# Attention over a graph batch: row factors split in fp16, turned by DMA and spread by TensorE with a constant; k's sums by VectorE

## The reference

```python
h = maximum(layernorm(x), 0)
q, k, v = heads(h @ Wq.T), heads(h @ Wk.T), heads(h @ Wv.T)
a = einsum('bhnd,bhmd->bhnm', q, k) * D ** -0.5 + 2 * adj      # adj is passed twice as bias
row_nonzero = any(a != 0, axis=-1)
p = softmax(where(row_nonzero, a, -inf));  p = where(isnan(p), 0, p)
o = einsum('bhnm,bhmd->bhnd', p, v)
out = x + o.reshape(B, N, D) @ Wo.T
```

## Time and profile before

| | |
|---|---|
| median of 3 runs | 1008.4 us (1008.09 to 1008.94) |
| the profiled execution | 1011.04 us, of which its span (first to last instruction) is 1009.2 us |
| PE busy | 967.0 us, 96% |
| ACT busy | 926.8 us, 92% |
| POOL busy | 861.7 us, 85% |
| DVE busy | 853.0 us, 85% |
| DMA, share of 16 engines | 98.1% |
| mean granted clock of TensorE | 0.988 of 2.4 GHz |

### The profile page before, as it was taken

How to read it: one execution, slowest core, us unless ns; L and a number is a source line. 1 busy time by engine, 2 the same in 40 slices (tenths; PEclk the granted TensorE clock), 3 DMA queues, 4 the chain that set the end, 5 groups by cost and what they waited for, 6 DMA issues and landing times.

```text
span 1009.2 us, 33752 instructions
## 1 busy us (share of the span) xinstructions
PE 967.0 (96%) x11596; PEld 666.3 (66%) x11596; DVE 853.0 (85%) x3090; ACT 926.8 (92%) x3025; POOL 861.7 (85%) x936
## 2 busy tenths in 40 slices
PE   6788999999999999999999999999999999999965
PEld 5566766676776667677666777666677766667632
DVE  6778988889898888989888898988889898888863
ACT  3399999999999999999999999999999999999992
POOL 1178989899988989998898999989899988989894
PEclk9899999999999999999999999999999999999988
DMA  6088999999999999999999999999999999999995
GB/s 250 11 145 144 190 188 188 183 193 200 179 190 189 189 188 192 187 199 184 185 182 194 188 201 187 185 194 175 193 192 195 177 196 183 190 188 176 172 178 117
DMA packets 569579, 182.59 MB, mean 181 GB/s; under 512 B 542784, under 2 KB 550976, under 8 KB 569408
## 3 DMA queue, kind: packets, MB, share of 16 engines
q1 hardware_dynamic: 569408, 180.43, 98.1%
HBM read 29.36 MB, written 16.78 MB: 46 GB/s over the span
## 4 chain that ended last, share of the span: by engine, by line
PE 58%; DVE 27%; issue 8%; ACT 5%; POOL 2%; DMA 1%; DVEq 0%; POOLq 0%; ACTq 0%; SPq 0%
PE ps L978 36%; DVE logits L690 14%; PE ps L1046 8%; PE ps L996 7%; DVE stats L595 4%; PE ps L861 3%; ACT probs L509 3%; DVE q_lo L753 2%; DVE o_norm L720 2%; PE ps L1022 1%; DVE some L708 1%; DVE w_max L610 1%; ACT p L522 1%; PE ps L950 1%; POOL p L411 1%
## 5 line engine op out<-in xcount | busy, mean ns | idle before, releaser
L411 POOL TENSOR_TENSOR p<-probs,p 128x512 f16<-128x512 f32 x512 | 586.5, 1162 | 95.8 <-ACT p L522 95.6
L509 ACT ACTIVATE probs<-logits,row_min 128x256 f32<-128x256 f32 x1024 | 514.3, 513 | 1.3 <-DVE row_min L690 1.3
L690 DVE CUSTOM_DVE_ANT_0 logits<-ps,adj_s,sigma 128x256 f32<-128x256 f32 x1024 | 438.0, 475 | 9.8 <-PE ps L996 9.7
L522 ACT ACTIVATE p<-probs 128x512 f16<-128x512 f32 x512 | 324.2, 633 | 0.0
L978 PE MATMUL ps<-ht_hi,w_hi 128*128 128x256 f16 x1024 | 280.9, 274 | 6.4 <-DVE w_lo L650 1.9
L978 PE MATMUL ps<-ht_lo,w_hi 128*128 128x256 f16 x1024 | 280.2, 274 | 0.0
L978 PE MATMUL ps<-ht_hi,w_lo 128*128 128x256 f16 x1024 | 280.1, 274 | 0.0
L509 ACT ACTIVATION_READ_ACCUMULATOR probs<-logits,row_min 128x1 f32 x1024 | 211.4, 206 | 0.0
L978 PEld LDWEIGHTS ps<-ht_hi,w_hi 128*128 128x128 f16 x1024 | 100.4, 98 | 34.3 <-DVE q_lo L753 11.4
L978 PEld LDWEIGHTS ps<-ht_lo,w_hi 128*128 128x128 f16 x1024 | 100.6, 98 | 14.5
L978 PEld LDWEIGHTS ps<-ht_hi,w_lo 128*128 128x128 f16 x1024 | 100.6, 98 | 12.0
(11 more groups left out here) (88 smaller groups left out, 1654.9 us busy)
## 6 DMA issues: line engine op xcount, KB each, us to landing
xs<-in_x SPq DMA_DIRECT2D x32, 512.0 KB, 4.5
out<-xs SPq DMA_DIRECT2D x64, 256.0 KB, 2.9
adj_raw<-in_adj SPq DMA_DIRECT2D x32, 256.0 KB, 3.6
pt<-p SPq DMA_TRANSPOSE x256, 4.1
w_nat<-p SPq DMA_TRANSPOSE x256, 3.3
w_nat<-in_L_gnn_Wq SPq DMA_DIRECT2D x1, 1024.0 KB, 6.3
w_nat<-in_L_gnn_Wk SPq DMA_DIRECT2D x1, 1024.0 KB, 9.1
w_nat<-in_L_gnn_Wv SPq DMA_DIRECT2D x1, 1024.0 KB, 11.2
```

Source lines behind the costliest of these rows:

```text
L411: g.tensor_tensor(p16[:, c % 2, k, 1], probs[:, h % 4].rearrange("p u n -> p (u n)"), p16[:, c % 2, k, 0], ALU.subtract).then_inc(p_split, 1)
L509: e = a.activation(probs[:, h % 4, u, :], logits[:, h % 4, u, :], ACT.Exp, bias=row_min[:, t.par(d), u, h:h + 1], scale=-1.0, accum_out=ro ...
L522: a.activation(p16[:, c % 2, k, 0], probs[:, h % 4].rearrange("p u n -> p (u n)"), ACT.Copy)\
L690: v.tensor_tensor_reduce(out=logits[:, h % 4, u, :], in0=ps[:, S_BANK + h % HC, N * u:N * u + N], in1=adj_s[:, t.par(d), u, :], scale=sigm ...
```

## The change

The row factors are finished by VectorE. `invert` runs twice for each batch, not four times (steps 7 and 15), over eight heads: `recip`, `some`, their product times 2^14 (`factor`), its fp16 part, and the fp16 rest, each waiting for the one before. Both parts lie side by side in `factor16[:, p, :]` (128 columns of fp16, of which 64 stay zero). A DMA transpose turns this into `factor16_t`, and TensorE multiplies it with a constant `spread` matrix (2^-14 where feature row and factor belong together), which adds the two parts and spreads them in the same matmul: four fp16 matmuls in the place of four fp32 transposes. GpSimd's `spread_norm` is gone. The constant is built once at the start by VectorE (18 memsets), turned by TensorE and copied by ScalarE.

`k_hi` is now written by one 512-wide activation for each job, without accumulating. VectorE sums the finished `k_hi` (128x1024 fp16) at step 12, GpSimd's `k_diag` moves from step 11 to step 13, TensorE's `row_test` from 13 to 15, and VectorE's `test_rows` from step 15 to step 1 of the next slot.

```diff
@@ sync @@
+            def turn_factor(t, d, p):
+                sp.wait_ge(factor_split, 2 * t.batch(d) + p + 1)
+                need(sp, aux_full, aux_after("norm", t.batch(d) - 1, p) if t.batch(d) else 0)
+                sp.dma_start_transpose(factor16_t[:, p, :], factor16[:, p, :]).then_inc(factor_in[p], 16)
+
             def slot(t):
                 for s in range(H):
                     turn(t, s - 1)
+                    if s == 0 and t.prev:
+                        turn_factor(t, -1, 1)
+                    if s == 8 and t.cur:
+                        turn_factor(t, 0, 0)
@@ gpsimd @@
-                    if s == 0 and t.prev:
-                        spread_norm(t, -1, NC - 1)
-                    if s % 4 == 0 and s >= 4 and t.cur:
-                        spread_norm(t, 0, s // 4 - 1)
...
-                    if s == 11 and t.nxt:
-                        pool.wait_ge(pj_hi, 4 * t.batch(1) + 4)
+                    if s == 13 and t.nxt:
+                        pool.wait_ge(k_summed, t.batch(1) + 1)
@@ scalar @@
             def take_k(t, g):
                 act.wait_ge(pj_full, pj_full_at(t, 2 + g))
-                for c in range(2):
-                    e = a.activation(k_hi[:, t.par(1), 2 * g + c, :], ps[:, PJ_BANK + g, N * c:N * c + N], ACT.Copy,
-                                     scale=DOWN, accum_out=k_sum[:, 2 * g + c:2 * g + c + 1])
-                e.then_inc(pj_hi, 1)
+                a.activation(k_hi[:, t.par(1), 2 * g:2 * g + 2, :],
+                             ps[:, PJ_BANK + g, :].rearrange("p (c n) -> p c n", c=2), ACT.Copy,
+                             scale=DOWN).then_inc(pj_hi, 1)
@@ vector @@
-            def invert(t, d, c):
+            def invert(t, d, p):
...
                 v.reciprocal(recip[:], row_sum[:, t.par(d), :, hs]).then_inc(norm_step, 1)
                 v.scalar_tensor_tensor(out=some[:], in0=row_min[:, t.par(d), :, hs], scalar=0.0,
                                        in1=some_qk[:, t.par(d), :, hs], op0=ALU.not_equal, op1=ALU.max)\
                  .then_inc(norm_step, 1)
+                dve.wait_ge(norm_step, 4 * done + 2)
+                v.scalar_tensor_tensor(out=factor[:].rearrange("p (u h) -> p u h", u=NU), in0=recip[:], scalar=NORM_UP,
+                                       in1=some[:], op0=ALU.mult, op1=ALU.mult).then_inc(norm_step, 1)
+                dve.wait_ge(norm_step, 4 * done + 3)
+                n = 2 * NU * HC
+                v.tensor_copy(factor16[:, p, 0:n], factor[:]).then_inc(norm_step, 1)
+                dve.wait_ge(norm_step, 4 * done + 4)
+                v.tensor_tensor(factor16[:, p, n:2 * n], factor[:], factor16[:, p, 0:n], ALU.subtract)\
+                 .then_inc(factor_split, 1)
...
+            def sum_k(t):
+                dve.wait_ge(pj_hi, 4 * t.batch(1) + 4)
+                v.tensor_reduce(out=k_sum[:], in_=k_hi[:, t.par(1)], axis=AX.X, op=ALU.add).then_inc(k_summed, 1)
...
-                    if s % 4 == 3 and t.cur:
-                        invert(t, 0, s // 4)
+                    if s % 8 == 7 and t.cur:
+                        invert(t, 0, s // 8)
...
-                        if s == 15:
-                            test_rows(t)
+                        if s == 12:
+                            sum_k(t)
+                    if s == 1 and t.cur:
+                        test_rows(t.batch(0))
@@ tensor @@
             def turn_norm(t, d, p):
-                pe.wait_ge(norm_ready, NC * t.batch(d) + 2 * p + 2)
+                pe.wait_ge(factor_in[p], 16 * (t.batch(d) + 1))
                 pe.wait_ge(aux_taken, aux_before("norm", t.batch(d), p))
                 for i in range(2):
                     for u in range(NU):
-                        m = tr(ps[:, AUX_BANK, N * i + P * u:N * i + P * u + P],
-                               norm[:, i, u, :], ident[:])
+                        m = mm(ps[:, AUX_BANK, N * i + P * u:N * i + P * u + P], spread[:, NU * i + u, :],
+                               factor16_t[:, p, :], start=True, stop=True)
...
-                    if t.nxt and s == 13:
+                    if t.nxt and s == 15:
                         row_test(t)
```

More of the change, by code:

```diff
@@ L28 @@
 K_SUM_DOWN = 1.0 / N
+NORM_UP = 2.0 ** 14
 Y_C = ()
@@ L125, in emit @@
         some_qk = sb("some_qk", [P, 2, NU, H])
-        some = sb("some", [P, NU, HC])
-        recip = sb("recip", [P, NU, HC])
-        norm = sb("norm", [P, 2, NU, P])
+        some = sb("some", [P, NU, 2 * HC])
+        recip = sb("recip", [P, NU, 2 * HC])
+        factor = sb("factor", [P, 2 * NU * HC])
+        factor16 = sb("factor16", [P, 2, P], F16)
+        factor16_t = sb("factor16_t", [P, 2, P], F16)
+        spread = sb("spread", [P, 2 * NU, P], F16)
         o_norm = sb("o_norm", [P, 2, N])
@@ L852, in _ @@
             pe.wait_ge(ident_set, 1)
+            pe.wait_ge(spread_set, 2 * NU * HC)
+            for i in range(2 * NU):
+                m = tr(ps[:, PJ_BANK, P * i:P * i + P], logits[:, 0].rearrange("p u n -> p (u n)")[:, P * i:P * i + P],
+                       ident[:])
+            m.then_inc(spread_turned, 1)
             def turn_h(t, d, k):
@@ L965, in project @@
                         pe.wait_ge(aux_taken, aux_after("h", t.batch(1), 1))
+                    if j == 0 and t.first:
+                        pe.wait_ge(spread_taken, 1)
                     if j == 6:
```

54 lines of the change are left out of this document (32 added, 22 removed).

## The result

The changed kernel takes 1099.95 us, the median of four runs (1088.11, 1090.90, 1108.99 and 1154.22); the kernel before, timed beside it, 1008.67 (1008.09 to 1009.77). The ratio is taken from the two runs near 1090 alone, since the other two stand over 1.5% above them; it is 1.0779, 95% interval 1.0747 to 1.0811. The profiled execution is that of 1088.11 us, its span 1086.3, against 1011.04 and 1009.2 before: 77.1 us more.

A forecast was written before the change was run, and what follows sets the result against it. A 29.5 us loop over TensorE, ScalarE and VectorE was taken to bound each slot; 3.1 - 0.4 = +2.7, times 31 = +84 us, took 1011.0 to 1095, or 1092 in the runs' median terms; range 1035 to 1125.

The forecast's parts named there:

- The holds at step 15: VectorE's `factor`, cast and subtraction in `invert` each wait for a GpSimd instruction: +3.1 us a slot; three holds given 0.47.
- My first rival: Two holds instead of three at step 15, one split less, 1.13 us a slot: 1057 us; chance 0.27.
- `neg_mean`, -0.4: VectorE's `neg_mean` may no longer be held: 0.4 us a slot gained, or up to 0.6 lost.
- ScalarE's 0.5: ScalarE's k activations, 512 wide without reads, save twice 0.25 us before `v_hi` (1): the loop gains 0.5 a slot.
- `invert` at step 7: VectorE's same three holds are possible, but GpSimd waits for ScalarE there: taken as 0, upper bound about 1 us.
- TensorE's part of the loop: Fp16 matmuls replacing transposes save 0.4 us a slot, none within the loop's 5.6 us; only `residual` comes earlier.
- `test_rows`: It moves from one place of VectorE's stretch to another: 0.
- k's sum, 0: VectorE's sum at step 12, 1.2 us, fits where it stood idle before `v_lo` (1): 0, bounds 0 and 0.5.
- The transposes, 0, bounds 0 and 1: Two more DMA transposes a slot on SP; step 8's should land about when TensorE reaches it: 0, bounds 0 and 1.
- The clock: TensorE's idle time could let its clock fall, up to 3 us a slot; not expected, as the gap is split.
- The rival of no hold: No holds to speak of at step 15: 1003 us; chance 0.09 together with TensorE's bound of 987.
- The case of more than three holds: `some` also meets `o_lo`, 1.1 us a slot more, 1127 us; or the clock falls, up to 3; chance 0.12.

The follow-up runs named there:

- Experiment 1: Kernel before, plus three dependent small products of two SBUF inputs on VectorE behind `some` at step 15, results unused: 1100.85 us, ratio 1.0899.
- experiment 2: Kernel before, plus three dependent small one-input reductions on VectorE behind `some` at step 15, results unused: 1047.88 us, ratio 1.0376.
- experiment 8: Changed kernel with `factor`, its fp16 part and rest on GpSimd, and SyncE issuing the factors' transposes of steps 0 and 8 earlier: 1025.91 us, ratio 1.0139.
- experiment 4: Changed kernel with `factor` written straight in fp16, cast and subtraction left out: 1053.30 us, ratio 1.0422.
- experiment 7: Changed kernel with the factors' transpose of step 8 issued ahead of the head's transpose beside it: 1081.15 us in one run, 1154.21, 1155.99 and 1157.30 in the others.
- experiment 10: Kernel before with the k part of the change alone, and `neg_mean` and `var_s` moved from VectorE to GpSimd: 1002.83 us, ratio 0.9923.
- Experiment 5: Kernel before with the k part of the change alone, row factors as before: 1037.26 us, ratio 1.0269.

## Why the prediction was right

Forecast 1092 us, measured 1099.95 as the median, and 1088 and 1091 for the two fastest runs. The profiled execution was to take 1095 and took 1088.1. Step by step:

- **The holds at step 15** (three, +3.1 with the earlier arrival): the mechanism is shown. Experiment 1 makes the loss out of three small products alone, experiment 2 takes the hold away with the second input, experiment 8 takes the chain away and most of the loss with it (with SyncE's order changed too). The size was off by one hold: two in a typical slot; three came in the first batch's alone (1.12, 1.08, 1.18 us). I had put `factor` at 0.20 behind `some` and `o_lo` 0.1 ahead of it; in fact `some` and `factor` follow at 0.16 and 0.15, and `o_lo` came 0.02 behind. My first rival named this case, with a miss "by under 0.1 us". By the count of holds that rival came true, and not the forecast; it priced the whole at 1057.
- **`neg_mean`, -0.4**: the step that had the wrong sign. It was held for longer, not less: +0.22. Everything around it was to move by 2 us, so its new place against GpSimd's splits was open; I had left it a bound of +0.6 for that, and no row spoke for -0.4. In experiment 4 it takes 0.17 in the slots of 28.94 and up to 0.81 in the others of the same run.
- **ScalarE's 0.5, `invert` at step 7, TensorE's part of the loop, `test_rows`**: right; -0.47, 0, 0, 0. At step 7 of a typical slot all five instructions took 0.82 us together, with GpSimd idle for most of it. In the second pattern (experiment 7) three of them are held there.
- **k's sum, 0**: right in the changed kernel, with experiment 10 behind it; VectorE still waits 1.17 us for `k_hi` (1) in each typical slot. Experiment 5 shows how narrowly: the k part alone costs 2.7%, by where it puts `neg_mean` and `test_rows`.
- **The transposes, 0, bounds 0 and 1**: right in the typical slot, and I missed a consequence. At 0.43 us late, one of them goes with four holds in place of two. The small transposes landed 2.3 us after their issue (median of 64; 2.2 to 4.5), those of step 8 2.6, the eight times larger ones 4.0. The late one had taken 3.1, no more than others before typical slots (up to 3.8); it had been issued 32.7 us after the one of the slot before, in place of 31.6. The one ahead of the four holds at 750.48 took 4.0, and TensorE's weight load waited 0.61 us for it.
- **The clock**: I had seen the gap split in two and expected it to stay up. So it does in the 22 typical slots. It falls in the slots with four holds, where one gap is 2.9 to 3.25 us, and in every slot of the second pattern, where it is 2.60. The first two slots have a low clock too (0.89 and 0.81), as in the kernel before (0.89 and 0.95).
- **The sum**: 31 x 2.12 would be 66, 18 below the 84 of the forecast; the nine uneven slots, 6.8 more than at 2.12 each, and the end, 5.2 against "0 to +3", gave part of it back. So the time is nearer to the forecast than its terms are: step 15 was 1.2 a slot too large, `neg_mean` 0.6 too small, and the irregular slots I had as a rival only. That these offset each other is luck; the sign, the place and the mechanism of the loss are not.

The rival of no hold needed GpSimd idle at step 15; between `o_hi` and the fourth split behind `o_lo` it paused for 0.08 us. The case of more than three holds was priced at 1127 for all slots, and with the clock at up to 3 us a slot more. The traces show it in four slots of the run of 1088, and in all from the second batch's on in experiment 7's run of 1157.

GpSimd is 65 us less busy (861.7 to 796.5), not 79.

What stays open: what decides in which pattern a run starts, and what starts an irregular slot where no transpose is late. Issuing the transpose earlier (experiment 7) did not keep the kernel out of the second pattern. No run isolates what sets the changed kernel's times of 1109 and 1154 apart from its others, or experiment 7's three of 1154 to 1157 from its 1081.

## What to carry to other kernels

A small VectorE instruction that takes two inputs from SBUF, or a cast or `tensor_scalar` there, cost in a chain here not its own 0.2 us but the rest of the GpSimd instruction that it met, each link anew; put such chains on GpSimd itself (0.20 to 0.22 us a step here), write them as a reduction where that is possible, or place them where GpSimd waits. Read these holds off the durations, since no view of waits has them. And price a shift of such an engine by all small instructions behind it, not by the edit: where a slot's time depends on an order decided by 0.02 us, give a range for both sides.
